# Turning the normalised rows between two attentions: float16 parts and DMA transposes in place of f32 transposes on TensorE

## Time and profile before

| | us |
|---|---|
| three runs | 1928.65, 1927.22, 1925.53 (median 1927.22) |
| span of the profiled execution | 1927.3 |
| busy in it: TensorE, GpSimd, ScalarE, VectorE | 1854.3, 1597.5, 1548.5, 1443.6 |
| the stretch between the attentions | 1201 to 1277 |

### The profile page before, as it was taken

One profiled execution on the slowest core, in us unless ns is written; L12 is line 12 of the kernel. 1 busy time (PEld: TensorE's weight loads), 2 busy tenths in 40 slices (PEclk: granted clock), 3 DMA queues, 4 the chain that ended last, 5 costly groups with the idle time before them and its releaser, 6 DMA issues.

```text
span 1927.3 us, 55726 instructions
## 1 busy us (share of the span) xinstructions
PE 1854.3 (96%) x23471; PEld 1256.4 (65%) x23471; DVE 1443.6 (75%) x2647; ACT 1548.5 (80%) x1921; POOL 1597.5 (83%) x1025
## 2 busy tenths in 40 slices
PE   4899999999999999999999998779999999999998
PEld 3566666666666666666666665547777777767766
DVE  7798878878878878878878875566767767767652
ACT  4799999999999999999999999646666666666664
POOL 3899999999999999999999999358688787787752
PEclk8999999999999999999999999889999999999999
DMA  6101100100100100100100100100000000000000
GB/s 148 35 11 26 34 15 22 35 17 20 35 19 18 35 19 18 35 19 17 35 23 14 35 2 2 55 1 2 2 1 2 2 2 2 2 1 1 2 2 23
DMA packets 45034, 37.96 MB, mean 20 GB/s; under 512 B 8304, under 2 KB 44144, under 8 KB 44528
## 3 DMA queue, kind: packets, MB, share of 16 engines
q1 hardware_dynamic: 44304, 34.00, 7.0%
q10 hardware_dynamic: 480, 0.39, 0.1%
HBM read 8.15 MB, written 1.05 MB: 5 GB/s over the span
## 4 chain that ended last, share of the span: by engine, by line
PE 87%; DVE 4%; POOL 3%; issue 3%; ACT 2%; DMA 0%; SPq 0%; POOLq 0%; DVEq 0%; ACTq 0%
PE ST L1639 11%; PE ST L1640 11%; PE RING L1520 7%; PE OO L1601 6%; PE OO L1603 6%; PE OO L1600 6%; PE OO L1520 4%; PE ST L1832 3%; PE ST L1838 3%; PE ST L1837 3%; PE ST L1839 3%; POOL PBUF L704 2%; PE OO L1859 2%; PE OO L1861 2%; PE OO L1863 2%
## 5 line engine op out<-in xcount | busy, mean ns | idle before, releaser
L620 POOL TENSOR_TENSOR PAB<-PR,PAB 128x1024 f16<-128x1024 f32 x342 | 724.3, 2134 | 42.3 <-ACT PAB L799 42.2
L799 ACT ACTIVATE PAB<-ST,exp_scale 128x1024 f16<-128x1024 f32 x512 | 567.6, 1109 | 0.0
L1104 DVE TENSOR_REDUCE maxes<-RING 128x1 f32<-128x512 f32 x661 | 439.6, 684 | 122.6 <-PE RING L1520 118.2
L1600 PE MATMUL OO<-VP,PAB 128*128 128x66 f16 x4096 | 446.6, 192 | 2.9 <-POOL PAB L620 2.9
L1601 PE MATMUL OO<-VP,PAB 128*128 128x64 f16 x4096 | 447.1, 193 | 0.0
L1603 PE MATMUL OO<-VP,PAB 128*128 128x66 f16 x4096 | 445.1, 192 | 0.0
L797 ACT ACTIVATE PR<-ST,exp_scale 128x1024 f32<-128x1024 f32 x342 | 381.9, 1117 | 64.7 <-PE ST L1640 61.8
L1600 PEld LDWEIGHTS OO<-VP,PAB 128*128 128x128 f16 x4096 | 380.2, 96 | 78.3 <-issue 15.5
L1601 PEld LDWEIGHTS OO<-VP,PAB 128*128 128x128 f16 x4096 | 377.0, 97 | 60.6
L1639 PE MATMUL ST<-QL,KH 128*128 128x512 f16 x1024 | 388.6, 380 | 2.0 <-DVE QH L1116 1.0
L1640 PE MATMUL ST<-QH,KL 128*128 128x512 f16 x1024 | 388.8, 380 | 0.0
(11 more groups left out here) (319 smaller groups left out, 4027.8 us busy)
## 6 DMA issues: line engine op xcount, KB each, us to landing
KH<-HS SPq DMA_DIRECT2D x124, 64.0 KB, 2.0
QL<-HS SPq DMA_DIRECT2D x64, 64.0 KB, 2.0
QL<-LS SPq DMA_DIRECT2D x64, 64.0 KB, 2.0
QH<-HS SPq DMA_DIRECT2D x64, 64.0 KB, 2.0
KL<-LS SPq DMA_DIRECT2D x62, 64.0 KB, 2.0
X<-in_L_attn_a_x SPq DMA_DIRECT2D x4, 256.0 KB, 4.2
SHARED<-in_rope_cos SPq DMA_DIRECT2D x1, 1024.0 KB, 5.2
SHARED<-in_rope_sin SPq DMA_DIRECT2D x1, 1024.0 KB, 7.3
```

The source lines that it names most:

```text
L620: pool.tensor_tensor(PB[:, s, :], PRA[g % PR_SLOTS], PA[:, s, :], ALU.subtract).then_inc(p_low_ready, 1)
L799: act.activation(PA[:, step % SLOTS_A, :], ST[step % 2][:, :], ACT.Exp, scale=scale).then_inc(sa.exps, 1)
L1104: dve.reduce_max(maxes[:, i // BLOCKS, i % BLOCKS:i % BLOCKS + 1], bank[:, :], X_AXIS).then_inc(sa.ring_taken, 1)
L1600: pe.matmul(o, high, v[:, 0:V2_AT], start=(m == 0 and qt == 0), stop=False, skip_group_check=True)
```

## The change

The transposes of the turn leave TensorE. ScalarE casts the rows of a block as they lie, XN to XNH (`high_rows`), VectorE subtracts as they lie, giving XNL (`low_rows`), and SP transposes each part of each block by DMA straight into XH and XL: eight transposes of 128 x 512 float16 elements. SP first waits until all hidden layers of the first F are made, since XH and XL lie over XNT. XNH and XNL lie in buffers that are idle there. `project_lead(b)` waits for both transposes of its block. On TensorE `ffn_out(0, 3)` stands ahead of `project_lead(0)`. On VectorE `low_rows(b)` stands right behind `settle_ffn(b)`. On ScalarE `high_rows(b)` stands right behind `normalise` of block b.

```diff
@@ tiles
-        TURN_B = [O[0], QUARTER[0], QUARTER[1], O[0]]
+        XNH = LS[:, :, :].rearrange("p a q -> p (a q)")
+        XNL = wo_squares[:, :].bitcast(F16)
@@ SP
+            sp.wait_ge(hid_put, BLOCKS * CH)
+            for b in range(BLOCKS):
+                q = slice(b * BLK, (b + 1) * BLK)
+                sp.wait_ge(xn_high, b + 1)
+                sp.dma_start_transpose(XH[:, q].rearrange("p (t c) -> p t c", c=P), XNH[:, q]
+                                       ).then_inc(xt_moved[b], 16)
+                sp.wait_ge(xn_low, b + 1)
+                sp.dma_start_transpose(XL[:, q].rearrange("p (t c) -> p t c", c=P), XNL[:, q]
+                                       ).then_inc(xt_moved[b], 16)
@@ ScalarE
+            def high_rows(b):
+                act.wait_ge(xn_ready, 2 * BLOCKS + b + 1)
+                act.activation(XNH[:, b * BLK:(b + 1) * BLK], XN[:, b * BT:(b + 1) * BT, :].rearrange("p a c -> p (a c)"),
+                               ACT.Copy).then_inc(xn_high, 1)
             normalise(3 * BLOCKS, 0, X, xn_ready)
+            high_rows(0)
             for j in range(1, CH):
                 relu(0, 3, j)
             deviations(3 * BLOCKS + 1)
-            high_block(2 * BLOCKS, TURN_B[0])
             normalise(3 * BLOCKS + 1, 1, X, xn_ready)
+            high_rows(1)
             deviations(3 * BLOCKS + 2)
             normalise(3 * BLOCKS + 2, 2, X, xn_ready)
-            high_block(2 * BLOCKS + 1, TURN_B[1])
+            high_rows(2)
+            deviations(3 * BLOCKS + 3)
             lead_part(0)
             lead_part(1)
-            deviations(3 * BLOCKS + 3)
-            high_block(2 * BLOCKS + 2, TURN_B[2])
             normalise(3 * BLOCKS + 3, 3, X, xn_ready)
+            high_rows(3)
             lead_part(2)
             lead_values(0)
             lead_part(3)
-            high_block(2 * BLOCKS + 3, TURN_B[3])
             lead_part(4)
@@ VectorE
+            def low_rows(b):
+                dve.wait_ge(xn_high, b + 1)
+                q = slice(b * BLK, (b + 1) * BLK)
+                dve.tensor_tensor(XNL[:, q], XN[:, b * BT:(b + 1) * BT, :].rearrange("p a c -> p (a c)"), XNH[:, q],
+                                  ALU.subtract).then_inc(xn_low, 1)
             settle_ffn(0)
+            low_rows(0)
             settle_ffn(1)
-            low_block(BLOCKS + 1, 0, TURN_B[0])
+            low_rows(1)
             settle_ffn(2)
+            low_rows(2)
             dve.wait_ge(bweights, 16 * 6)
             take_block_b(0)
-            low_block(BLOCKS + 2, 1, TURN_B[1])
             settle_ffn(3)
-            low_block(BLOCKS + 3, 2, TURN_B[2])
+            low_rows(3)
             take_block_b(1)
             take_lead_values(0)
-            low_block(BLOCKS + 4, 3, TURN_B[3])
             take_block_b(2)
@@ TensorE
             def project_lead(b):
-                pe.wait_ge(xnt_ready, 2 * BLOCKS + b + 1)
+                pe.wait_ge(xt_moved[b], 2 * 16)
-            turn_x(8)
             ffn_out(0, 2)
             pe.wait_ge(hid_ready, BLOCKS * CH)
             pe.wait_ge(swapped_ready, 2)
+            ffn_out(0, 3)
             project_lead(0)
-            turn_x_b(1)
-            ffn_out(0, 3)
-            turn_x_b(2)
             project_lead(1)
             values_lead(0)
-            turn_x_b(3)
             project_lead(2)
```

More of the change, by code:

```diff
@@ L444, in build @@
         xnt_ready = sem("xnt_ready")
+        xn_high = sem("xn_high")
+        xn_low = sem("xn_low")
+        xt_moved = [sem(f"xt_moved{b}") for b in range(BLOCKS)]
         wt_put = sem("wt_put")
@@ L927, in last_block @@
             def last_block(b):
-                act.wait_ge(xnt_put, 3 * BLOCKS + b - 1)
+                act.wait_ge(xnt_put, 2 * BLOCKS + b - 1)
                 act.activation(XNT[:, b * BLK:(b + 1) * BLK], O[0][:, :], ACT.Copy).then_inc(xnt_ready, 1)
@@ L1707, in hidden @@
             def hidden(r, b):
-                pe.wait_ge(xnt_ready, BLOCKS + b + 1 if r == 0 else 3 * BLOCKS + b - 1)
+                pe.wait_ge(xnt_ready, BLOCKS + b + 1 if r == 0 else 2 * BLOCKS + b - 1)
                 for j in range(CH):
@@ L1774, in max_b @@
                           start=(c < qb), stop=True, skip_group_check=True).then_inc(sbb.ring_put, 1)
-            def turn_x_b(b):
-                pe.wait_ge(xn_ready, 2 * BLOCKS + b + 1)
-                turn_block(2 * BLOCKS + b, b, TURN_B[b])
             def project_lead(b):
-                pe.wait_ge(xnt_ready, 2 * BLOCKS + b + 1)
+                pe.wait_ge(xt_moved[b], 2 * 16)
                 q = slice(b * BLK, (b + 1) * BLK)
@@ L1942, in _ @@
                 pe.wait_ge(xn_ready, 3 * BLOCKS + b + 1)
-                wait(pe, xnt_ready, 3 * BLOCKS + b - 2)
-                turn_block(3 * BLOCKS + b, b, O[0])
+                wait(pe, xnt_ready, 2 * BLOCKS + b - 2)
+                turn_block(2 * BLOCKS + b, b, O[0])
                 hidden(1, b)
```

## The result

The changed kernel took **1936.37 us**, median of 4 runs (1932.07 to 1937.07), against 1927.93 for the kernel before, also 4 runs. The ratio is 1.004, interval 1.0028 to 1.0052: slower by some 8 us. The profiled execution took 1936.76 us with a span of 1934.9, 7.6 more than before.

The account below looks back on a forecast made before the run. TensorE was taken to bound the attentions, VectorE's taking of lead block 1 and GpSimd's run the changed passage. 4.4 for later scores plus 0.7 for the clock gave 5.1 on 1927.3: 1932.3 us, range 1927.5 to 1938.

Parts of the forecast that it names:

- Slower, by about 5 us: Whole kernel: later scores plus 4.4 and clock plus 0.7 make 5.1 us; slower than measurement can confuse, chance 0.68.
- Nothing later gives the time back: Behind the start of the scores at 1277 the program is the same, so a later start ends later by as much.
- The holds: VectorE, before the scores: low parts wait for ScalarE's casts with takings queued behind; scores start 4.4 us later overall.
- GpSimd's distance: GpSimd on the lead's later blocks: runs without a gap at 4.64 us a block, against 5.64 before, giving 1.0 back.
- The transfers: Eight DMA transposes on SP: landing in 1.9 to 6.6 us, hidden at zero cost; chance 0.10 that they become the bound.
- D in the sense of the formula: Time per transpose if run one after another: scores shift by 8D - 25.0, exceeding 4.4 from D = 3.7 on.
- The clock: TensorE idle from 1258.3 to 1264.3 drops to 1.2 GHz, slowing block 1's items until about 1268: plus 0.7 us.
- The clock stays low longer: Rival: TensorE stays at half clock to 1275, so scores start at 1284.5, plus 7.5 us, 1934.7; chance 0.15.
- The clock gives back: Rival: half clock at the maxima and first scores vanishes, returning 3.8 us; shift 0.6, 1927.8; chance 0.15.
- Faster: Rival: VectorE still takes block 1 of the lead at 1257.9; 3.5 us plus clock gain 1.5 come off, 1922.2; chance 0.05.
- the removed pieces: TensorE's turns, ScalarE's casts from a bank and VectorE's old subtractions: at most 3.5 us on the path before the scores.

Follow-up runs that it names:

- c_after: The changed kernel run again without any edit, beside the other runs on one chip: median 1933.22 us, ratio 1.0027 to the kernel before.
- x4: Changed kernel with TensorE's pauses filled by matmuls into an idle bank that nobody reads: 1929.87 us, ratio 1.0009 to the kernel before.
- y2: Kernel before the change, with TensorE's pauses filled by matmuls nobody reads: 1925.54 us, ratio 0.9988 to the unfilled kernel before.
- z1: Changed kernel with VectorE taking block 1 of the lead ahead of low part 3: 1931.92 us, ratio 1.0017 to the kernel before.
- z2: Changed kernel with low parts 0 and 1 behind the takings of blocks 1 and 2 of F: 1930.18 us, ratio 1.0008 to the kernel before.
- y0: Changed kernel with all low parts reordered on VectorE and two lead casts moved ahead of block 3's root on ScalarE: 1926.09 us, ratio 0.999 to the kernel before.
- y1: The order of y0 with TensorE's pauses also filled by matmuls nobody reads: 1924.27 us, ratio 0.998 to the kernel before.
- x2: Changed kernel with each transpose made twice, the second issued only after the first landed: 1936.23 us, ratio 1.0042 to the kernel before.
- x2b: Changed kernel with each transpose issued twice side by side, the copy into idle memory, TensorE waiting for all: 1932.81 us, ratio 1.0028 to the kernel before.
- x1: Changed kernel with each low part put back where the old low part stood in VectorE's program: 1930.26 us, ratio 1.0011 to the kernel before.

## Why the prediction was right, point by point

- **Slower, by about 5 us**: 1932.3 was forecast, 5.1 above 1927.2. The first measurement gave 1936.37, 8.4 above its kernel before, the larger repeat 1933.22, 4.8 above; both lie in the range, the first near its upper end. That 4.8 is so near 5.1 is in part luck, for one kernel's runs spread over 8 us. What stands is the sum up to the scores, 4.72 in c_after against 5.1. "Nothing later gives the time back" held in the first profile and not in c_after, which got 0.51 and 1.57 back later.
- **The holds.** The order of events came out as written (times from the start of the last hidden layers). VectorE's first low part waited until 1242.86, output 2 came 5.32 behind the hidden layers (forecast 1243.75 - 1238.38 = 5.37), output 3 at 11.25 (forecast 11.27), and VectorE waited 2.86 for the last cast (forecast 2.9). Block 1 of the lead was taken 26.13 behind the hidden layers in the first profile; in c_after, with output 3 at full clock, at 24.64, where 25.20 had been added up. Size: 4.13 at full clock against 4.4. GpSimd's start on block 1 moved by 5.12 (26.01 behind the hidden layers in x4, 20.89 in y2) and not by the 5.65 added up; smaller terms went the other way. z1, z2 and y0 show it to be these holds: without the last 2.4 go, without the first two 2.6, without all 5.75 (5.05 at full clock, x4 against y1: 4.13 over before, and the 0.92 that the change then gives). y0 and y1 also put two casts of ScalarE back; what these are worth alone was not run.
- **GpSimd's distance** of 4.6 was forecast for a run without a gap. In the first profile it is 5.35 and 4.75, in c_after 5.48 (1264.54 to 1270.02) and 4.75. The 1.0 that this run was to give back came only in part: block 1's two sums arrive one at a time, since TensorE's items lie at half clock there and the second waits for VectorE. At full clock, in x4, the sums are 4.69 and 4.67 apart: the forecast holds, and the rest was the clock's.
- **The transfers** were hidden. The nearest rows, moves of half the size, gave 1.9 to 6.6; measured were 2.4 to 3.8 to landing and 1.19 to 1.32 to issue, twice the issue of a move. A block's two parts are issued 1.24 apart (1.67 in block 0) and overlap, so D in the sense of the formula is far below 3.7. x2, with D = 4.01, fits the point from which they decide, and that it was not reached is shown by x2b. The Trainium skill, "Advanced Engine Details and Errata", section "X-Bar Transpose (TRN2)", calls them as fast as regular transfers. In landing this case is near it, 128 KB in 2.5 where 64 KB by a plain move took 2.0; in issue it is not, with twice the time. The figure in the Trainium skill, "VectorE: DVE Perf Modes", section "The three transpose paths", multiplied by four gave an estimate of 5.2 a part; four 128x128 in one transfer took 2.5.
- **The clock was under-sized: this is the step that was off.** I had put 0.7 on it, for the pause from 1258 that makes block 1's items slow, and that came as written (half clock from about 1263.8 to 1270.6, and matmuls of 0.63 where 0.38 is usual). What I did not see is that the two waits ahead of outputs 2 and 3, which I had worked out myself as 1.5 and 2 us of idle TensorE, can take the clock down as well: in the first profile output 3 ran 1.6 longer for it (5.44 against 3.81). In c_after the clock took 4.72 - 4.13 = 0.59 more than in the kernel before ahead of the scores, against the 0.7 forecast. In the first profile it took 6.09 - 4.13 = 1.96 there, and with 0.50 from before the passage, 4.13 of holds and 1.07 behind the scores that makes the 7.6. Whether the two pauses bring the clock down differs from execution to execution: x2, x2b and z1 have the same 1.72 and 2.09 as c_after and, like it, output 3 at 3.81; of these five profiles the first alone shows it. It may be a spread as much as a cost. From lowest to highest run, kernels with both pauses differ by 8.0, 7.9 and 7.2 us (c_after, z1, x2b; 4.0 in the five runs of x2), those without by 1.8 to 5.8, filled or not (y1 1.8, z2 2.3, x4 5.3, y0 5.8). That goes with the pauses, but no run isolates it.
- **The rivals.** "The clock stays low longer" (to 1275) did not happen as put, the clock was back at about 1270.6; but its size, 7.5, is what the first run lost, by a low stretch in another place. "The clock gives back" did not happen: the maxima and first scores lay at half clock again. That this gain was there to be had, y1 and y2 show (24.33 from scores to steady before, 21.19 in both), only not for free. Faster: its mechanism, the removed pieces with VectorE's holds costing nothing, is y0, and there it gave 1.03 up to the scores (0.92 at full clock, y1 against y2), not 3.5. In y0 GpSimd starts on block 1 only 0.2 earlier than before (20.66 against 20.89 behind the hidden layers) and then runs without a gap, so there is little left to gain; that it is GpSimd's pace that holds the rest is read from the trace and was not tested.

Open: why the same pauses of 1.72 and 2.09 bring the clock down in some executions and not in others; no run settles it. Nor was the difference of 1.57 at the end of the second attention followed up.

## What to carry to other kernels

Work that is moved off an engine because it is cheap there may need its inputs at another place in two other in-order queues: write down what stands behind the moved instruction on its new place, and move that ahead of it, before counting what was saved. Where a change makes new pauses on TensorE, even of 1.7 and 2.1 us as here, count the clock under the work that follows, as something that may or may not come, and not only behind the longest pause. Filling such pauses with matmuls nobody reads was worth as much here (0.9988 on the kernel before) as the change in its best order (0.999).

## What the runs showed of the hardware

- **A subtraction on VectorE with both inputs in SBUF and GpSimd's instructions hold each other up.** y0, then z1:

```profile
1255.06 1.17 DVE L1387 TENSOR_TENSOR wo_squares<-XN,LS 128x512 f16<-128x512 f32 x1
```

```profile
1261.81 1.37 DVE L1387 TENSOR_TENSOR wo_squares<-XN,LS 128x512 f16<-128x512 f32 x1 [0.47 <-ACT LS L839]
```

It takes 0.69 alone, and GpSimd's instruction beside it 1.60 in y0 instead of 1.16; in x1 it took as much as 1.51. The last low part of y0 kept to 0.72, and GpSimd's sum beside it took 1.71 instead of 1.27. The times fit turns: in z1 GpSimd's first sum ends at 1262.64, VectorE at 1263.18, and GpSimd's next, begun at 1262.59, only at 1264.30. The old low part, one input of which lay in a bank of PSUM, took 0.69 at 1262.95 in the kernel before with GpSimd busy. So forming the parts in SBUF has a price that the change's own order hides, since its low parts run while GpSimd rests; y0 and z1 pay it.
- **Transposes in flight overlap.** They are issued 1.24 us apart and land 2.5 after their issue. Eight of 128 KB cost nothing when doubled side by side (x2b) and 2.1 us when half of them wait for one another (x2).
- **Useless matmuls kept the granted clock at 1.00** through a passage of 60 us in which TensorE was busy for 47 in the kernel before (54 with them, in y1 and y2); the first scores then took 21.19 instead of 24.33 us.
